# Attention 2 of a sandwich block: queries projected turned over, causal mask added on VectorE, rows normalised on GpSimd

## What is computed

```python
x = x + layernorm(attn(layernorm(x), Wq, Wk, Wv, Wo))      # attention 1: 4 x 256 tokens, 16 heads of 16
# attention 2, on h = rmsnorm(layernorm(x)): 32 query heads and 4 key/value heads of 128
q, k = rope(h @ Wq), rope(h @ Wk);  v = h @ Wv
scores = where(causal, q @ k.T / sqrt(128), -1e9)
o = softmax(scores) @ v;  x2 = resid + o @ Wo
# 32 experts (top 8) and a shared one on rmsnorm(x2); then x + layernorm(...)
```

## Time and profile before

| | us |
|---|---|
| three runs, median (lowest to highest) | 1034.11 (1030.66 to 1034.36) |
| the profiled execution, own time | 1029.21 |
| its span, first to last instruction | 1027.0 |
| what lies around the span | 2.2 |
| mean granted TensorE clock | 0.969 |

### The profile page before, as it was taken

How to read it: one execution, slowest core, us unless ns; L and a number is a source line. 1 busy time by engine, 2 the same in 40 slices (tenths; PEclk the granted TensorE clock), 3 DMA queues, 4 the chain that set the end, 5 groups by cost and what they waited for, 6 DMA issues and landing times. The chain is left out here.

```text
span 1027.0 us, 20816 instructions
## 1 busy us (share of the span) xinstructions
PE 935.8 (91%) x6296; PEld 834.4 (81%) x6296; DVE 693.8 (68%) x1608; ACT 582.9 (57%) x1571; POOL 393.5 (38%) x362
## 2 busy tenths in 40 slices
PE   3799999468899999999999999997989999999995
PEld 2699998357788888888888888886878888888884
DVE  7356666647788888787888888886545454454446
ACT  4788887545566566666666665665433333333333
POOL 5633333255445545545545544420022222222221
PEclk9899999788999999999999999999899999999998
DMA  6001000200000300003000000100143333333331
GB/s 196 22 1 43 20 22 1 93 20 1 1 2 20 113 20 20 20 0 112 20 20 20 20 1 20 36 1 2 30 155 107 107 107 107 107 107 108 111 102 41
DMA packets 41846, 52.96 MB, mean 52 GB/s; under 512 B 3888, under 2 KB 34224, under 8 KB 41808
## 3 DMA queue, kind: packets, MB, share of 16 engines
q1 hardware_dynamic: 40720, 51.44, 15.0%
q10 hardware_dynamic: 1088, 1.05, 0.3%
HBM read 41.86 MB, written 1.18 MB: 42 GB/s over the span
## 5 line engine op out<-in xcount | busy, mean ns | idle before, releaser
L1255 POOL TENSOR_TENSOR b_sin_part<-b_raw,rope_sb 128x512 f32<-128x512 f32 (+1 forms) x96 | 114.7, 1195 | 93.6 <-ACT b_raw L1211 93.6
L551 ACT ACTIVATE b_prob<-banks,b_negmax 128x128 f32<-128x128 f32 (+1 forms) x256 | 104.1, 425 | 17.0 <-DVE b_negmax L592 17.0
L592 DVE TENSOR_REDUCE b_negmax<-banks 128x1 f32<-128x128 f32 (+1 forms) x256 | 76.4, 349 | 54.6 <-PE banks L488 50.0
L1266 POOL TENSOR_TENSOR b_q_row<-b_cos_part,b_sin_part 128x512 f32<-128x512 f32 x64 | 82.1, 1283 | 76.0 <-DVE b_cos_part L1230 69.1
L1748 ACT ACTIVATE moe_hid<-banks 128x512 fp32r<-128x512 f32 x66 | 39.5, 598 | 126.0 <-DVE banks L1839 126.0
L608 DVE TENSOR_SCALAR b_prob<-b_prob,b_rsum 128x128 f32<-128x128 f32 (+1 forms) x256 | 106.5, 477 | 2.3
L1832 DVE TENSOR_TENSOR moe_gated<-banks,moe_share 128x512 f32<-128x512 f32 x66 | 45.6, 691 | 88.5 <-PE banks L75 83.5
L1187 ACT ACTIVATE b_qt<-banks 128x512 fp32r<-128x512 f32 x64 | 38.4, 599 | 90.5 <-PE banks L1107 90.5
L73 PE MATMUL banks<-b_w,b_ot 128*128 (+1 forms) x256 | 77.9, 304 | 12.5 <-DVE b_ot L1163 12.5
L488 PE MATMUL banks<-mask,ident 128*128 128x128 bf16 x384 | 88.4, 233 | 0.0
L617 POOL TENSOR_TENSOR a_prob<-a_prob,a_rsum 128x256 f32<-128x256 f32 x64 | 51.6, 827 | 85.7 <-DVE a_rsum L599 85.7
(11 more groups left out here) (227 smaller groups left out, 3250.4 us busy)
## 6 DMA issues: line engine op xcount, KB each, us to landing
moe_share<-gates SPq DMA_DIRECT2D x32, 512.0 KB, 3.6
b_src_t<-act_t SPq DMA_DIRECT2D x13, 512.0 KB, 2.9
b_w_raw<-in_b_wq SPq DMA_DIRECT2D x4, 1024.0 KB, 5.7
b_w_raw<-in_b_wo SPq DMA_DIRECT2D x4, 1024.0 KB, 7.7
a_src_t<-act_t SPq DMA_DIRECT2D x5, 512.0 KB, 2.9
moe_w_raw<-in_wg SPq DMA_DIRECT2D x16, 128.0 KB, 2.1
moe_w_raw<-in_wu SPq DMA_DIRECT2D x16, 128.0 KB, 2.2
moe_w_raw<-in_wd SPq DMA_DIRECT2D x16, 128.0 KB, 2.3
```

The lines of the kernel that those rows point to most:

```text
L551: last = nc.scalar.activation(self.prob[:, p, h, lo:lo + width], m.s_ps[:, h, lo:lo + width], ACT.Exp, bias=self.negmax[:, p % 2, t, h:h + 1],
L592: last = nc.vector.tensor_reduce(self.negmax[:, p % 2, t, h:h + 1], m.s_ps[:, h, lo:lo + width], AX, ALU.max, negate=True)
L1255: nc.gpsimd.tensor_tensor(out, x, factor, ALU.mult).then_inc(self.sin_ready, 1)
L1266: nc.gpsimd.tensor_tensor(out, self.cos_part[:, par, 0:n], self.sin_part[:, par, 0:n], ALU.add).then_inc(self.rotated, 1)
```

## The change

Attention 2 is written anew; the rest stays, but for the mask of attention 1 and small additions in `prepare`.

- The queries of a pair are projected with the weights as the stationary operand, so that they come out turned (head dimension on the partitions, 256 tokens along the row): 12 matmuls of 256 columns per pair in place of units of 512, and no transposes. `pe_queries(P+3)` runs in slot P.
- Rotation of turned queries: ScalarE copies the bank to `raw`, two transfers of SyncE (64 partitions each, 256 KB together) exchange the halves of the partitions into `swp`; VectorE makes the cosine product from the bank, GpSimd the sine product in place and the sum in place. ScalarE and VectorE split it; both now read SBUF.
- The tables are turned once in `prepare` and multiplied by -1, so that the scores are negated. No mask matmul: VectorE adds `mask_neg` (0 or +1e30) in place in PSUM with `tensor_tensor_reduce`, which also gives the row minimum; the exponential has scale -1.
- GpSimd scales the probabilities (two instructions a pair), VectorE only makes the reciprocal.
- Keys and values keep their row form, with a bank (`qt_ps`) and buffers of their own. The activations are read in place, and `src_t` is gone.
- No hardware loops in attention 2: all 64 slots are written out.
- In attention 1, one mask matmul of 2 x 128 columns ahead of two rows of scores takes the place of one behind each.

```diff
@@ prepare
+            nc.gpsimd.affine_select(out=m.mask_neg[:], in_=m.mask_neg[:], compare_op=ALU.is_ge, fill=-NEG, ...)
             nc.gpsimd.memset(m.b_w[:, 2 * B_W:4 * B_W].bitcast(F32), 0.0)
+            for k in range(2):
+                for t in range(NTT):
+                    last = nc.tensor.transpose(w_bank(0)[:, k, t * PART:(t + 1) * PART], m.rope[:, k, t, :], m.ident[:])
+            nc.scalar.activation(m.rope_t[:], w_bank(0), ACT.Copy, scale=-1.0)
@@ Attention.pe_scores (attention 1 alone now)
+            nc.tensor.matmul(self.diagonals(h), m.ident16[:], self.mask_twice(), start=True, stop=False, ...)
             for t in range(NTT):
-                self.pe_score(out, it, p, h, t, width)
-                last = nc.tensor.matmul(diagonal, m.ident16[:], m.mask[:], start=False, stop=True)
+                last = self.pe_score(m.s_ps[:, h, lo:lo + width], it, p, h, t, width)
@@ AttentionB
+    POOL_NORMALISES = True
+    def pe_queries(self, pe, P):
+        if P >= 2:
+            wait(pe, self.raw_ready, P)
+            wait(pe, self.cos_ready, P)
+        for h in range(2):
+            out = self.q_bank(P)[:, h * SEQ:(h + 1) * SEQ]
+            for c in range(NC):
+                at = c * B_QKV + (2 * p + h) * DH
+                last = three(nc, out, self.w_at(it, 0, at, DH), self.w_at(it, 1, at, DH),
+                             self.src(it, 0, c, 0, SEQ), self.src(it, 1, c, 0, SEQ), c == 0, c == NC - 1)
+    def act_raw(self, act, P):
+        wait(act, self.q_full, P + 1)
+        wait(act, self.swapped[P % 2], self.SWAPPED * (P // 2))
+        nc.scalar.activation(self.raw[:, P % 2, :], self.q_bank(P)[:], ACT.Copy).then_inc(self.raw_ready, 1)
+    def sp_swap(self, sp, P):
+        wait(sp, self.raw_ready, P + 1)
+        wait(sp, self.q_added, P - 1)
+        for to, of in ((0, half), (half, 0)):
+            sp.dma_start(self.swp[to:to + half, P % 2, :], self.raw[of:of + half, P % 2, :]).then_inc(...)
+    def dve_cos(self, dve, P):
+        wait(dve, self.raw_ready, P + 1)
+        nc.vector.tensor_tensor(self.pairs_of(self.cos_part, P), self.q_bank(P)..., self.q_table(0), ALU.mult)
+    def pool_rotate(self, pool, P):
+        wait(pool, self.swapped[P % 2], self.SWAPPED * (P // 2 + 1))
+        nc.gpsimd.tensor_tensor(sin, sin, self.q_table(1), ALU.mult).then_inc(self.sin_ready, 1)
+        wait(pool, self.cos_ready, P + 1)
+        wait(pool, self.sin_ready, P + 1)
+        nc.gpsimd.tensor_tensor(total, total, self.swp[:, P % 2, :], ALU.add).then_inc(self.q_added, 1)
+    def act_queries(self, act, P):
+        wait(act, self.q_added, P + 1)
+        nc.scalar.activation(self.qt[:, P % PAIRS, 0, :], self.cos_part[:, P % 2, :], ACT.Copy).then_inc(self.qt_hi, 1)
+    def dve_queries(self, dve, P):
+        wait(dve, self.qt_hi, P + 1)
+        nc.vector.tensor_tensor(self.qt[:, P % PAIRS, 1, :], self.cos_part[:, P % 2, :], self.qt[:, P % PAIRS, 0, :]..., ALU.subtract)
+    def dve_max(self, dve, p, P):
+                last = nc.vector.tensor_tensor_reduce(
+                    row, row, m.mask_neg[:, SEQ - width:SEQ], 1.0, -NEG, ALU.add, ALU.min,
+                    accum_out=self.negmax[:, p % 2, t, h:h + 1])
+    def slot_pe(self, pe, P):      # scores P, kv, project P-5, values P-4, KT, queries P+3, prob_t P-2
+    def slot_act(self, act, P):    # prob_t P-3, queries P+1, exp P, kv, outputs P-4, KT, raw P+3, values, weights
+    def slot_dve(self, dve, P):    # max P, prob_t P-3, queries P+1, reciprocal P-1, kv, outputs P-4, KT, cos P+3, values, add
+    def slot_pool(self, pool, P):
+            self.pool_normalise(pool, (P - 1) % PAIRS, P - 1)
+            self.pool_rotate(pool, P + 2)
+            self.pool_kv(pool, it + 1, ...)        # slots 1 and 2
+            self.pool_weights(pool, it)            # slot 3, iterations 0 to 11
@@ AttentionB.build, SyncE
-            with sp.Fori(1, KV - 1) as g:
-                load_batch(NB * g, 0)
...
+            for P in range(self.STAGES):
+                if slot > 0 and slot % (PAIRS * NB) == 0 and ...:      # slot = P - 3
+                    load_weights(slot // (PAIRS * NB) + 1)
+                self.sp_swap(sp, P)
```

More of the change, by code:

```diff
@@ L782, in pe_score @@
         at = h * SEQ + t * PART
-        self.m.nc.tensor.matmul(out, self.qt[:, p % 2, 0, at:at + PART], self.keys(it, p, width),
-                                start=True, stop=False)
+        return self.m.nc.tensor.matmul(out, self.qt[:, p % 2, 0, at:at + PART], self.keys(it, p, width),
+                                       start=False, stop=True, skip_group_check=True)
     def pe_values(self, pe, it, p, P):
@@ L1079, in pe_unit @@
[L1079 removed]
+                last = nc.tensor.transpose(bank[:, t * PART:(t + 1) * PART], self.k_row[:, t, :], self.m.ident[:])
+            last.then_inc(self.kv_full, 1)
             return
[L1081 removed]
+        t = u
         wait(pe, self.w_ready, 4 * (it // NB) + 3)
[L1084 to L1090 removed]
@@ L1091, in pe_unit @@
[L1091 to L1109 removed]
+        if u == self.KV0:
+            wait(pe, self.kt_ready, it)
+        elif it:
+            wait(pe, self.k_raw_ready, NTT * it + 1)
@@ new lines, in slot_pool, with slots @@
+    def slot_pool(self, pool, P):
+        it, p = P // PAIRS, P % PAIRS
+        if self.runs(P - 1):
+            self.pool_normalise(pool, (P - 1) % PAIRS, P - 1)
+        if self.runs(P + 2):
+            self.pool_rotate(pool, P + 2)
+        if it + 1 < self.ITS and p in self.ROPE_AT:
+            self.pool_kv(pool, it + 1, self.ROPE_AT[p])
+        if p == PAIRS - 1 and self.more_weights(it):
+            self.pool_weights(pool, it)
+    TAIL = 7
+    def slots(self, eng, slot, plan):
+        for P in range(self.STAGES + self.TAIL):
+            slot(eng, P)
+            for stage, b in plan.get(P - self.STAGES, ()):
+                stage(b)
@@ L1398, in _, with work @@
-            for k in range(self.DRAIN, self.TAIL):
-                self.tail(plan, k)
+            self.slots(pe, self.slot_pe, {
+                4: ((turn_h2, 0), (turn_h2, 1), (turn_h2, 2), (route, 0)),
+                5: ((turn_h2, 3), (route, 1)), 6: ((route, 2),)})
         @block.scalar
         def _(act):
-            def work(s, units=behind(act, self.act_unit)):
-                units(s)
+            def work(s):
+                if s == 3:
+                    self.act_kv(act, 0, self.KV0)
+                    self.act_kv(act, 0, self.KV1)
```

559 lines of the change are left out of this document (311 added, 248 removed).

## The result

The changed kernel takes 973.37 us (median of 972.09, 972.82, 973.91 and 2943.49) against 1034.23 before (1030.66 to 1034.54): a ratio of 0.9415 [0.9387, 0.9443]. The execution of 2943 us, at full granted clock, is left out of the ratio, and nothing here explains it. Forecast were 984 us in a range from 958 to 1009, and faster. The profiled execution took 973.91 us with a span of 972.0, which is 55.0 less than the span before.

A forecast was written before the change was run, and what follows sets the result against it. TensorE was taken to bind, at 30.4 us an iteration. Gains of 32.4 (12 iterations with a split), 15.4 (3.5 others) and 2 elsewhere make 50 us off 1029.2, so 979; with 4.9 to the median, 984 us, range 958 to 1009.

The forecast's parts named there:

- TensorE after: TensorE's work in attention 2 without mask matmuls and query transposes: 26.0 us an iteration, 4.4 less than before.
- VectorE after: VectorE in attention 2 loses the scaling and gets the fused row minimum: about 20.2 us an iteration, from 25.1.
- Rival (b): VectorE binds attention 2, the row minimum costing double: 7.2 us a slot, 1007 us; chance 0.22.
- The ring: Attention 2's chain of reciprocal, GpSimd scaling and rotation, ScalarE query copy, VectorE low part: 6.2 us a slot, 27.7 with split.
- The collision with the split: In attention 2, VectorE's low part of the queries waits for GpSimd's weight split: 2.0 us in each of 12 iterations.
- rival (a): TensorE alone binds attention 2, with iterations of 26 us throughout: 70 us gained, 964 us; chance 0.20.
- 27 to 28 us while weights are split: Sign in the next profile that the forecast is right: length of attention 2's iterations that hold a weight split.
- about 26 in the last four: Sign in the next profile that the forecast is right: us per iteration in attention 2's last four, without splits.
- A granted clock under full speed in the middle of attention 2: Listed as a sign that the prediction was wrong in kind, beside TensorE waiting for turned probabilities; no size given.
- The loads ahead of the exchange: Two groups' weight loads ahead in SyncE's queue delay attention 2's exchanges, mostly inside 3.2 us of slack: 1 us in all.
- up to 4 us late: Lateness taken for attention 2's exchange each of the two times a group's weight loads stand ahead in SyncE's queue.
- Exchange, preparation, attention 1, fetching: Exchange lands after 2.9 us; preparation loses 1 us; attention 1 gains 4; fetching straight code nothing, bound 10 either way.

The follow-up runs named there:

- the run with two passes: Changed kernel with the row minimum taken as an addition of the mask in place, then a plain reduction: 983.47 us, 0.9543 of the kernel before.
- the load on GpSimd: Changed kernel with one extra GpSimd addition over 128x256 a slot, ahead of each rotation: 995.22 us, 0.9652 of the kernel before.

## Why the prediction was right, and where it was not

- **TensorE after: right.** 26.0 us an iteration forecast, 25.7 measured (25.6 where no weights are split); scores 1.46 for 1.43, projection 1.44 for 1.51, queries 1.42 for 1.51, values and turning as before. It was the 256-column matmul that was priced a little high: 1.42 / 12 = 0.118 us in the queries, for 0.126 from the earlier trace rows.
- **VectorE after: right.** 20.7 us for 20.2. The minima were to cost a subtraction plus 0.17. Their distance from start to start is 0.38 us for 256 columns and 0.22 for 128; a pair takes 0.60, a pair of plain reductions (in the run with two passes) 0.52. The rule of the Trainium skill (VectorE: DVE Perf Modes, section Two Vector instructions with no wait between them) holds here in its count: 256 read-outs of 141 ns stand in the trace. They cost little, since each starts together with what stands behind it. Rival (b) falls with it: 0.46 and 0.31 us, not 0.8 and 0.6.
- **The ring: right in kind, a little long, and wrong in the one term that chose the case.** It was forecast at 6.2 us a slot. Scalings start at 380.44, 386.32, 392.40, 398.44 and 406.11: 5.88, 6.08, 6.04, and 7.67 with the split, 25.67 in all. The collision with the split is as described (the low part of the queries at 2.13 us, 992 ns on average for 0.69 without), but it adds 1.6 and not 2.0, and the slots with a key rotation take 0.2 us more than the one without, where 0.46 each were put down. Behind the rotations GpSimd still idles for 0.7 us. So the ring takes at most 25.7 us where 27.7 stood in the sum (about 25.4 by the estimate from the load on GpSimd), and "12 x (30.4 - 27.7)" should have read 12 x (30.4 - 25.7) = 56, 24 us more. In its plain iterations the kernel went as rival (a) said, though not with the ring out of the way: the runs with more work for either show all but a tie. The sign "27 to 28 us while weights are split" did not come; "about 26 in the last four" did.
- **The Trainium skill's rule on shared interfaces** (GPSIMD Engine Reference, section Key points) agrees with 688 ns becoming 992 when the input moved from PSUM into SBUF. The scaling, with one tensor as input, is held up too (1.01, 2.24 and 4.22 us for the same four); whether that is the page's other case, a 2-port mode, no run here shows.
- **The splits' place: missed.** The text listed GpSimd's split by its length and its collision, and did not ask who waits for it one slot later. That was 3 boundaries, 15.4 us over plain iterations, though the diff's slots say it. "A granted clock under full speed in the middle of attention 2" was named as a sign of an error in kind, and it was one.
- **The loads ahead of the exchange: mis-sized.** 1 us was taken; removing it gave 6.4. The slack of 3.2 was right (3.3 measured). The term that failed is the "up to 4 us late": the exchange came some 6.4 us late, and 3 us of wait stayed each time.
- **Exchange, preparation, attention 1, fetching: right.** 2.3 us for 2.9; 0.6 for 1; 3.1 to 3.9 for 4. The instruction queue moved 0.61 MB in place of 0.31, and no wait for it is seen in attention 2.
- **Scaling: right that it had to leave VectorE**, though its weight was not seen: without that one move the change is worth nothing. The prediction counted its 7.6 us of length, and not that it would stand in front of the keys while the split holds it up.

By the spans 50 us were forecast and 55.0 came. An error of 24 us on one side met two of 15 and 5 on the other, and smaller ones elsewhere, some 3 us gained in the first two iterations and 2.9 lost behind the last score among them: the nearness of the number is partly luck. The other half of the 11 us between 984 and 973.4 is the 4.9 us by which the profiled execution of before lay under its median; the changed kernel's lay 0.5 over. In the later sets the kernel before has medians of 1029.7 to 1030.3, and the gain beside it is 55.9 us (1029.70 and 973.82), not 60.9.

The lower end of the range, 958, is a small slip: with scores at 1.3 us, rival (a) would give 15.5 x 4.9 + 2 = 78, which is 956.

## What to carry to other kernels

When an instruction is moved by one slot, look up the first consumer of what it produces at the end of a group, not only its neighbours on its engine: a stall that comes three times hides in no average, and it costs more than its length when the clock falls behind it. When another engine's work holds an instruction up, ask what stands behind it in its queue: the wait can show up elsewhere. When an engine's chain is forecast a few per cent above another's, treat them as a tie and price both ways. A transfer that waits for an event in the same queue as short, urgent ones should be released early in a quiet slot, or stand in another queue.

## What was not expected of the hardware

- The instruction that reads out VectorE's accumulator (141 ns) starts at the same time as the next minimum: fused sum and minimum in place in PSUM take 465 and 313 ns, with 0.38 and 0.22 us between starts.
- After TensorE had stood still for 3.2 us, the granted clock was 0.51 for the next 5.8 us, with TensorE busy for 5.76 of them, and the stall cost 5.7 us; behind two other stalls of 3.1 to 3.2 us it was 0.71 and 0.72, and they cost 4.9 and 4.8.
- An exchange of halves of the partitions, 128 KB within SBUF, lands after 2.3 us, and after 7.8 and 7.9 us when 2.25 MB were issued ahead of it in its queue.
- Four scalings of 128 and 256 columns within SBUF on VectorE take 1.01 us while GpSimd idles and 4.22 us beside GpSimd's rotation and split.
